# Selective-scan stage of a fused four-layer network: seven product buffers instead of three, and a chunk's output projection issued two states into the next chunk

## The reference

```python
A_tilde = exp(dt[..., None] * A)                 # decay of state n
B_tilde = (A_tilde - 1) / (A + 1e-10)
h_t = A_tilde * h_(t-1) + B_tilde * u            # per feature and state n
y = einsum('bln,blen->ble', C_proj, h)           # sum over the 16 states
y_gated = (y + u * D) * silu(z)
h_residual = h_residual + y_gated @ W_out.T      # the output projection
```

## Time and profile before

| | us |
|---|---|
| median of three executions | 1682.14 |
| lowest, highest | 1678.66, 1684.33 |
| the profiled execution, its own time | 1694.94 |
| its span in the trace | 1693.1 |
| the scan stage in the span (first scan to the end of the last gate) | 149.9 to 371.3 |
| VectorE busy in the span | 795.0 |
| GpSimd busy in the span | 434.8 |
| TensorE, mean granted clock as a share of 2.4 GHz | 0.967 |

### The profile page before, as it was taken

The page is one execution under the profiler, slowest core; times in us unless marked ns, Lnnn a source line. Parts: engine busy times, 40 slices in busy tenths (PEclk is TensorE's granted clock), DMA queues, the critical chain, the costliest instruction groups (busy, mean ns, idle before and its releaser), DMA issues.

```text
span 1693.1 us, 22322 instructions
## 1 busy us (share of the span) xinstructions
PE 1561.7 (92%) x7798; PEld 1114.3 (66%) x7798; DVE 795.0 (47%) x1710; ACT 501.2 (30%) x983; POOL 434.8 (26%) x426
## 2 busy tenths in 40 slices
PE   5896898988899999999998999999999989998779
PEld 4542333448899999999996555778854445665664
DVE  3575798887111111111107773113766557667524
ACT  1246454441222221222214522113310025544210
POOL 0254687771111111111104000000010003222350
PEclk9998999998999999999999997999999999999889
DMA  5233554445355555321312002001000010001231
GB/s 177 63 104 98 138 126 105 110 92 179 126 193 212 212 205 195 121 82 51 147 44 78 1 0 84 0 1 50 1 1 0 1 50 1 11 1 38 89 108 63
DMA packets 63366, 142.13 MB, mean 84 GB/s; under 512 B 11244, under 2 KB 41605, under 8 KB 56549
## 3 DMA queue, kind: packets, MB, share of 16 engines
q1 hardware_dynamic: 56884, 122.46, 22.7%
q0 software_dynamic: 6368, 18.23, 3.3%
HBM read 205.26 MB, written 15.61 MB: 130 GB/s over the span
## 4 chain that ended last, share of the span: by engine, by line
PE 75%; DVE 13%; issue 3%; ACT 2%; POOL 2%; DMA 2%; SPq 1%; another core or an unknown queue 1%; DVEq 0%; POOLq 0%; ACTq 0%
PE psum L810 43%; PE psum L1134 9%; PE psum L842 7%; PE psum L905 4%; DVE work L1880 3%; PE psum L1050 2%; PE psum L820 2%; DVE work L2020 1%; DVE work L2019 1%; POOL work L2113 1%; PE psum L969 1%; DVE bst L1535 1%; PE psum L988 1%; DMA work<-in_txt 1%; PE psum L1174 1%
## 5 line engine op out<-in xcount | busy, mean ns | idle before, releaser
L810 PE MATMUL psum<-work 128*128 128x128 f32 (+3 forms) x3400 | 471.2, 300 | 15.6 <-DMA work<-in_xp 15.6
L810 PEld LDWEIGHTS psum<-work 128*128 128x128 f32 x3400 | 441.3, 193 | 32.5 <-DMA work<-in_xp 15.6
L1947 DVE TENSOR_TENSOR work<-sq,psum 128x512 f32<-128x512 f32 x82 | 56.3, 687 | 390.6 <-PE psum L810 390.6
L2113 POOL TENSOR_TENSOR work<-work,w_late 128x408 f32<-128x408 f32 (+1 forms) x160 | 162.4, 1050 | 53.9 <-DVE work L1880 24.4
L1880 DVE TENSOR_TENSOR_SCAN work<-psum,work 128x414 f32<-128x414 f32 (+1 forms) x160 | 159.7, 1060 | 34.5 <-POOL work L2113 22.6
L2077 POOL TENSOR_TENSOR rs<-rs,power 128x4 f32<-128x4 f32 (+3 forms) x40 | 44.4, 1112 | 480.3 <-DVE rs L1542 472.4
L905 PE MATMUL psum<-work,xn 128*128 128x408 f32 (+1 forms) x320 | 148.4, 575 | 15.9 <-POOL work L2113 15.4
L1134 PE MATMUL psum<-w_late,xn 128*128 128x512 f32 x352 | 153.9, 595 | 0.0
L2139 POOL DMA_INDIRECT y_rows<-sq,row_of x41 | 40.6, 990 | 361.7 <-ACT sq L1234 361.7
L1335 ACT ACTIVATE psum<-work,a_neg 128x408 f32<-128x408 f32 (+1 forms) x160 | 100.0, 627 | 105.2 <-DVE work L1880 105.2
L905 PEld LDWEIGHTS psum<-work,xn 128*128 128x128 f32 x320 | 53.6, 193 | 105.0 <-POOL work L2113 86.2
(11 more groups left out here) (284 smaller groups left out, 2097.1 us busy)
## 6 DMA issues: line engine op xcount, KB each, us to landing
work<-in_W SPq DMA_DIRECT2D x123, 1024.0 KB
w_late<-c_rows SPq DMA_DIRECT2D x48, 204.0 KB, 3.5
w_attn<-in_B SPq DMA_DIRECT2D x64, 128.0 KB, 2.5
w_late<-c_rows SPq DMA_DIRECT2D x32, 238.0 KB, 3.7
w_attn<-in_A SPq DMA_DIRECT2D x64, 64.0 KB, 2.2
w_attn<-in_A SPq DMA_DIRECT2D x32, 128.0 KB, 2.5
work<-y_rows SPq DMA_DIRECT2D x8, 512.0 KB, 6.9
w_late<-in_we SPq DMA_DIRECT2D x2, 2048.0 KB, 8.3
```

Source lines behind the costliest of these rows:

```text
L810: mm = pe.matmul(dst, lhs(k), rhs(k), start=(k == 0), stop=(k == parts - 1))
L1947: dve.tensor_tensor(hm[:, j % 2, 4 * q:4 * q + 4, :].rearrange("p k n -> p (k n)"), sa[:, i % 2], A.at(("e3", j, q)), ALU.mult).then_inc(s ...
L2113: pool.tensor_tensor(seqs(ym[:, g % RING, 0:ntok(c)]), f[:, :, 1:SEQ + 1], seqs(cbr[:, k % CRING, 0:ntok(c)]), ALU.mult).then_inc(sem("y_p ...
```

## The change

Three things are done. `ym` gets a ring of its own, YRING = 7 slots instead of RING = 3, and GpSimd's wait for `y_added` looks seven steps back instead of three; `f_buf` keeps its three slots. `out0(c - 1)` moves in TensorE's list from the end of chunk c - 1 to behind `yacc` of state n = 1 of chunk c (four steps, i = 0 to 3, and a `comp` step if one falls on that k); the last chunk's `out0` stays where it was. To match it, `w2c` moves from n = 2 to n = 3 and VectorE's `add_h` from after scan i = 6 to after scan i = 8. No instruction is added or taken away.

```diff
+YRING = 7
+OUT_N = 1
...
-        ym = carve(RING * NMAX).rearrange("p (r n) -> p r n", r=RING)
+        ym = carve(YRING * NMAX).rearrange("p (r n) -> p r n", r=YRING)
...
-            if n == 2:
+            if n == OUT_N + 2:
                 for m in range(HALVES):
                     CW.plan(("w2c", c, m), (sem("cw_used"), 2 * c + m + 1))
                 step("w2c", c)
             if k in UNIT_K:
                 plan_units(1)
-            if n == N_STATE - 1:
-                plan_h("out0", L0A, c, CW)
+            if n == OUT_N and c:
+                plan_h("out0", L0A, c - 1, CW)
+        plan_h("out0", L0A, CHUNKS - 1, CW)
...
-                    pe.matmul(dst[:, 0:ntok(c)], diag[:, m, n, :], ym[:, g % RING, 0:ntok(c)], start=(n == 0),
+                    pe.matmul(dst[:, 0:ntok(c)], diag[:, m, n, :], ym[:, g % YRING, 0:ntok(c)], start=(n == 0),
...
-                    if c and i == 6:
+                    if c and i == 2 * OUT_N + 6:
                         add_h(L0A, "out0", c - 1, CW, True)
...
-                    if g >= RING:
-                        pool.wait_ge(sem("y_added"), g - RING + 1)
+                    if g >= YRING:
+                        pool.wait_ge(sem("y_added"), g - YRING + 1)
...
-                    pool.tensor_tensor(seqs(ym[:, g % RING, 0:ntok(c)]), f[:, :, 1:SEQ + 1],
+                    pool.tensor_tensor(seqs(ym[:, g % YRING, 0:ntok(c)]), f[:, :, 1:SEQ + 1],
```

More of the change, by code:

```diff
@@ L249, in build @@
         f_buf = carve(RING * NS).rearrange("p (r n) -> p r n", r=RING)
-        ym = carve(RING * NMAX).rearrange("p (r n) -> p r n", r=RING)
+        ym = carve(YRING * NMAX).rearrange("p (r n) -> p r n", r=YRING)
         cbr = w_late[:, EXPERTS * HALVES * D // 2:][:, 0:CRING * NMAX].rearrange("p (r n) -> p r n", r=CRING)
         sp_a = sq[:, 0]
-        cursor[0] -= RING * (NS + NMAX)
+        cursor[0] -= RING * NS + YRING * NMAX
         dt_pos = full()
```

## The result

The changed kernel took 1667.18 us (median of 5 executions, 1665.00 to 1668.84), the kernel before 1681.68 us (median of 5, 1678.66 to 1684.33; the forecast's 1682.14 was the median of the first three of them). The mechanism at the chunk ends was right; the size was too small, and the range too narrow. A second measurement, further down, gave 11.5 us.

A forecast was written before the change was run, and what follows sets the result against it. The scan stage was taken to last as long as VectorE's work plus its idle time; 1.06 + 2.99 + 2.97 + 0.24 + 0.85 + 0.37 = 8.5 us off the median 1682.14 gave 1673.6 us, range 1668.5 to 1681.

The forecast's parts named there:

- The four terms of the chunk ends: VectorE's idle time won behind the gates between chunks 0 to 4: 1.06, 2.99, 2.97 and 0.24 us.
- the new wait at the end of chunk 3: VectorE waits 1.0 us for out0, behind a comp step at k = 65; of 1.24 us only 0.24 is won.
- `w2c` and `add_h` were free: At the chunk ends, moving these two was costed at nothing, with 2 us to spare for w2c.
- The C rows: Rival: GpSimd's 0.8 us waits after weight pairs reach VectorE; 7.5 of 8.5 us come back, 1681.1 us; chance 0.2.
- It does not do what it says: At the chunk ends, moving out0 frees TensorE only after the gate; the ring could do the work alone, sum unchanged.
- The ring alone, inside a chunk: Waits for yacc behind a comp step go with four more slots: 0.85 us near 195.88, 0.37 near 317.96.
- More goes than I counted: Rival: VectorE's other 1.6 us of waits for GpSimd and 0.4 from the first chunk go too; 1671.6 us, chance 0.12.
- the base of the sum: The 8.5 us counted in one profiled execution of 1694.94 us were taken off the runs' median of 1682.14 us.
- the rival of the half clock: TensorE at 1.2 GHz after the gates delays out0 and w2c, 16 us at two chunk ends; 1689.6 us, chance 0.07.
- In the chunk ends at 1.00: Said against TensorE falling to 1.2 GHz after the gates: its clock is 1.00 over the whole stretch from 207.5.
- the best case: Lower end of the range: the case of more gain, 1671.6 us, less the runs' scatter of 3 us, 1668.5.

The follow-up runs named there:

- kernel before + GpSimd: Kernel before with forty memsets of 16 columns added on GpSimd ahead of products i = 14, 16, ..., 28 of each chunk; ratio to before 1.0004.
- changed kernel + VectorE: Changed kernel with forty memsets of 16 columns added on VectorE ahead of scans i = 14, 16, ..., 28 of each chunk; ratio to before 0.9914.
- the ring alone: Kernel before with seven product buffers only; out0, w2c and add_h stay where they were; ratio to before 0.9936.
- five slots: Kernel before with five product buffers instead of three, TensorE's order as before the change; ratio to before 0.9924.
- changed + GpSimd: Changed kernel with forty memsets of 16 columns added on GpSimd ahead of products i = 14, 16, ..., 28 of each chunk; ratio to before 0.9920.
- the last version: Changed kernel with four scan buffers instead of three and comp of k = 65 behind out0; 1677.4 against 1695.1 us, ratio 0.9884.

## Why the prediction was wrong in size

**Right.** The bound was named rightly: VectorE's work plus its idle time at the chunk ends. The four terms of the chunk ends came to 7.8 us for 7.3 forecast, and the new wait at the end of chunk 3 was 1.00 us for 1.0. `w2c` and `add_h` were free, as costed. The C rows did not become the bound: VectorE's waits for GpSimd from chunk 1 on are 0.7 us. That either part could do the work alone was left open under "It does not do what it says", and it is so, for both.

**Wrong, the term "The ring alone, inside a chunk".** It took 0.37 us for chunks 1 to 4, and the insides gave 3.3. Two steps failed. First, only the wait at 319.09 was followed back to `yacc` behind a `comp` step and counted, while the listed waits inside fell by 1.9 us, 0.69 of it a wait for ScalarE that the sum left alone. The rival "More goes than I counted" had this in kind, with 1.6 us for the waits not named and a chance of 0.12. Second, the whole sum rests on listed idle time being all that can be won, and 1.4 us more went that no list shows: in chunk 1 a row of 22 scans without a listed wait was 0.57 us longer. Cutting the `comp` steps showed the gaps of chunks 1 and 4 to be their work; those of chunks 2 and 3 are open.

**Wrong in part, the base of the sum.** The 8.5 us were taken off the median as if the one trace stood for it ("so I take the same 8.5 us off the median"). The last gate of the kernel before ended at 371.2, 376.0 and 373.5 us in three traces, mean 373.6, and I had read the shortest. The changed kernel's ended at 359.0 and 359.6. The mean difference is 14.3 us. The 2.4 us between the first trace and the mean are 2.1 us of gate parts in which TensorE started at 1.2 GHz and 0.8 us inside chunks, less 0.6 us by an earlier first gate. That this is what the medians hold is argued and not shown: all three traces come from the slower level, and 14.3 stands near the 14.5 of the first measurement but above the 11.5 of the second.

**Wrong in sign, the rival of the half clock.** I put it into the changed kernel. It was in the kernel before, which rests TensorE for 2.24 to 2.66 us at the three later gates and then has only three products of cover. The changed kernel rests it for 0.7 to 1.4 us there, and in neither of its traces did the clock fall behind one of the first four gates. With the memsets on VectorE it fell behind two, and cost 0.9 and 1.1 us. "In the chunk ends at 1.00" was true of the one trace and was read as a property of the kernel.

**The range.** Its lower end was the best case less 3 us of scatter. It held no term for a base that varies by 4.8 us in the very stage that the change works on. How far the forecast missed is itself uncertain by chance: the changed kernel's median was 1667.2 us the first time, below the range, and 1670.7 the second, inside it, 11.5 us under its kernel before (by the interval 9 to 14).

## What to carry to other kernels

Where a ring feeds an in-order engine that also does long foreign steps, count the ring's cover in time against the longest such step, and look at the length of whole rows of work rather than at listed waits: small delays that no list shows add up. Before forecasting what a stall is worth, read the stage in more than one execution if TensorE rests there, since a clock that falls after the rest made the same stall 1.7 to 2.9 us longer here now and then, and not at all where the ring had five or seven slots. More buffers and an earlier place for the blocking step are two cures for one wait; try each alone before paying for both.

## What the runs showed of the hardware that was not expected

- A rest of 2.65 us at a gate was followed in some executions by a stretch at 1.2 GHz, in others by none, in the same kernel: of the six gate parts at the ends of chunks 2 and 3 in three traces of the kernel before, three were long, all with a mean clock of 0.61 to 0.77 behind the gate. At the end of chunk 1, with a rest of 2.24 us, the clock was 1.00 in all three, but it fell there in the kernel before + GpSimd, with the same rest. In the changed kernel + VectorE it fell once after 2.25 us and once after 1.36. The length of the rest alone does not decide it.
- With the ring alone and with five slots the clock fell behind all six of the later gates (mean 0.73 to 0.79), and no gate part was longer than 17.14 us.
- Less work on TensorE made it slower where it mattered: with the comp steps cut the mean clock behind three gates was 0.60, 0.60 and 0.76, and the gate parts grew by 2.7, 3.1 and 1.3 us.
- Forty small memsets, 4.5 us on GpSimd or 2.9 us on VectorE, left the insides of chunks 1 and 3 within 0.32 us of what they were. Neither engine's own pace is the bound in those long rows of scans, though VectorE is busy nearly all of them; what sets it was not found. In chunks 2 and 4 up to 0.7 us were felt.
- The phase from 1609 to 1651 us of the first trace is as long in changed kernels on the slower level: from the first to the last add of this phase (L2048 before, L2051 after) 42.0 us there, 41.5 and 41.8 in changed + GpSimd and in the last version, and 34.1 and 32.8 in the changed kernel's two traces on the faster level. What lengthens it is not known.
